# A hand-written order of work: v's copy behind the third turning's, the second exponentials behind the first, rank and x's addition between the maxima

## The chip, the cores and the metric
The kernel runs on one core of one Trainium2 chip. The metric is device time in microseconds of one execution: a median of several runs. One further execution was profiled.

## What is computed
A layer of cross attention followed by a mixture of experts, all in float32, for 16 batches of 256 tokens of width 256 and a context of 256 rows of width 192:
```python
def xattn(x, context, w_q, w_k, w_v, w_o, b_o):        # 16 heads of 64
    q, k, v = x @ w_q, context @ w_k, context @ w_v    # split into heads
    sim = einsum('bhid,bhjd->bhij', q, k) * 64 ** -0.5
    out = einsum('bhij,bhjd->bhid', softmax(sim), v)
    return out @ w_o + b_o
x = x + xattn(layernorm(x), ctx, ...)
x = x + ffn(layernorm(x), ...)
```
`ffn` takes a softmax over 8 experts, the two best of each token, a position for each token within its expert (a running count over all 4096 tokens, at most 640 per expert), an expert MLP 256 to 1024 to 256 with exact gelu, and the sum of both experts' rows weighted by the gates.

## The kernel before
**Attention part.** Work goes by *periods*: 64 of them, four to a batch, each with two pairs of heads, that is four heads (*units* 0 to 3) for all 256 queries. Batch `b` has periods `4b` to `4b + 3`; the text calls them its first to fourth. To keep float32's precision on TensorE most operands are split into a head and a rest, and a product is three products. So ScalarE copies each product out of PSUM (the head: `qh`, `kh`, `ah`, `xth`) and VectorE subtracts (the rest: `ql`, `kl`, `al`, `xtl`).

In period `m` these steps run, each on the engines named:
- `scores` (TensorE, L557): q times k for the four units into PSUM banks 0 to 3. `max0` to `max3` (VectorE, L896): one reduction for each unit. `exp0` to `exp3` (ScalarE, L739): two exponentials and two reads of the accumulated sum each, into `prob`.
- `inv0`, `inv1` (L901) and `norm0` to `norm3` (L907), VectorE: the probabilities over their sum. `inv1`, `norm2` and `norm3` run one period later.
- `turn0` to `turn3` of period `m - 1`: TensorE transposes the 256 x 256 probabilities of a unit (L573) into PSUM banks 4, 0, 1 and 4, and ScalarE copies them out into `probt` (L693). Banks 0 and 1 are those of the scores, so the turnings wait for the exponentials and the next scores wait for the copies.
- `pv` of period `m - 2`: probabilities times v (L587), copied to `ah`, its rest to `al`.
- `q`, `k` of period `m + 1` and `v` of period `m` (the last is a quarter of v, copied out by ScalarE only).
- per batch: `o` twice (the output product; VectorE adds `xin` and the sum is `x2`, L927), `xt` and `x2t` (transposes of the normalised tokens), and routing of a batch two or three behind: `ln2_stats`, `ln2`, `logits`, `bias`, `shift`, `gate` (L957 to L966), `rank` (L973 to L977), `pos` (TensorE, needs `rank`'s `chosen`), `slot`, `keys`, `pick`, and then four scatters by GpSimd to `slot_table` (L446).

**What sets the order.** Each engine runs its steps in the order of one list, `timeline()`, written by hand. An engine's queue is in order: an instruction that waits for a semaphore holds up all behind it. `xt`, `q`, `k`, `v`, `pv`, `o`, `x2t`, `logits` and `pos` share three PSUM banks (5 to 7) in turn, in the list's order, so each waits until the step three ahead of it has been read out by its last reader (`WORK_READ`; for `v` that is its copy, for `o` the addition). The wait that `scores` has on the turnings is
```python
if m >= 2:
    pe.wait_ge(sem("probt"), UNITS * (m - 2) + 3)
```
that is, the third copy of the turnings made in the period just before.

**Expert part.** After the last batch the rows of each expert are read from `slot_table`, transposed, multiplied by both weights (also split), weighted and added to the output by indirect DMAs.

Of the kernel before, what the change touches and what calls it, by code (L numbers as in the profile page):

```python
# [28 lines left out]
B, S, D = 16, 256, 256  # L29
# [4 lines left out]
ST = S // P  # L34
# [24 lines left out]
def timeline():  # L59

    out = [("ln1_stats", 0), ("ctx", 0), ("split", 0), ("ln1", 0), ("split", 1), ("xt", 0), ("q", 0), ("k", 0),
           ("split", 2), ("split", 3)]
    for m in range(PERIODS + 1):
        b, r = divmod(m, PER_B)
        live, turned, more = m < PERIODS, 1 <= m < PERIODS + 1, m + 1 < PERIODS
        out += [("scores", m), ("max0", m), ("max1", m), ("max2", m), ("max3", m), ("exp0", m)] if live else []
        scaled = [("inv1", m - 1), ("norm2", m - 1), ("norm3", m - 1)] if turned else []
        if m == PERIODS:
            out += [("ln2_stats", B - 2), *scaled]
            scaled = []  # L70
        out += [("pv", m - 2)] if m >= 2 else []
        out += [("exp1", m)] if live else []
        stats = [("ln2_stats", b - 2)] if r == 1 and 2 <= b < B else []
        if 3 <= b < B:
            out += {0: [("bias", b - 3)], 2: [("slot", b - 3)]}.get(r, [])
        if m == PERIODS - 1:
            out += [("bias", b - 2), ("shift", b - 2)]
        out += stats or scaled
        out += [("q", m + 1)] if more else []
        out += scaled if stats else []  # L80
        if 3 <= b < B:
            out += {0: [("shift", b - 3)], 2: [("keys", b - 3)]}.get(r, [])
        out += [("turn0", m - 1)] if turned else []
        out += [("exp2", m)] if live else []
        out += [("k", m + 1)] if more else []
        out += [("inv0", m), ("norm0", m), ("norm1", m)] if live else []
        out += [("turn1", m - 1)] if turned else []
        out += [("exp3", m)] if live else []

        out += {0: [("split", 4)], 1: [("split", 5)], 2: [("split", 6)], 3: [("split", 7)]}.get(m, [])  # L90
        out += [("v", m)] if live else []
        if r == 0 and b + 1 < B:
            out += [("ctx", b + 1)]
        if b == 0:
            out += {0: [("ln1_stats", 1)], 1: [("ln1", 1)]}.get(r, [])
        if 3 <= b < B:
            out += {0: [("gate", b - 3), ("rank", b - 3)], 3: [("pick", b - 3)]}.get(r, [])
        if r == 1 and 2 <= b < B:
            out += [("ln2", b - 2)]
        if r == 3 and b + 2 < B:  # L100
            out += [("ln1", b + 2)]
        out += [("turn2", m - 1)] if turned else []
        if r == (1 if b else 2) and b + 1 < B:
            out += [("xt", b + 1)]
        if r == 2 and 2 <= b < B:
            out += [("x2t", b - 2)]
        if r == 2 and b + 2 < B:
            out += [("ln1_stats", b + 2)]
        if r == 2 and 1 <= b < B:
            out += [("o", ST * (b - 1))]  # L110
        if r == 0 and 2 <= b < B:
            out += [("o", ST * (b - 2) + 1)]
        if r == 3 and 2 <= b < B - 1:
            out += [("logits", b - 2)]
        out += [("turn3", m - 1)] if turned else []
        if r == 2 and b == B - 1:
            out += [("logits", b - 2)]
        if m == PERIODS - 1:
            out += [("gate", b - 2), ("rank", b - 2), ("o", ST * (b - 1) + 1), ("pos", b - 2)]
        if r == 1 and 3 <= b < B:  # L120
            out += [("pos", b - 3)]
    last = B - 1
    out += [("slot", last - 2), ("ln2", last - 1), ("keys", last - 2), ("pick", last - 2),
            ("x2t", last - 1), ("pv", PERIODS - 1), ("logits", last - 1), ("bias", last - 1), ("shift", last - 1),
            ("gate", last - 1), ("o", ST * B - 2), ("rank", last - 1), ("o", ST * B - 1), ("ln2_stats", last),
            ("pos", last - 1), ("slot", last - 1), ("keys", last - 1), ("pick", last - 1), ("ln2", last)]
    out += [(stage, last) for stage in ("x2t", "logits", "bias", "shift", "gate", "rank", "pos", "slot", "keys",
                                        "pick")]
    assert len(set(out)) == len(out)
    return out  # L130
# [6 lines left out]


TIMELINE = timeline()
WORK_BANKS = 3  # L140

# [8 lines left out]
def build(nc, x, ctxt, wq, wk, wv, wo, bo, rw, rb, w1, b1, w2, b2, out):  # L150
    es = ExitStack()
    with es:
        sems = {}

        def sem(name):
            if name not in sems:
                sems[name] = es.enter_context(nc.semaphore("s_" + name))
            return sems[name]

        def sb(stack, name, shape, dt=F32):  # L160
            return stack.enter_context(nc.sbuf_tensor(name, [P, *shape], dt))
# [25 lines left out]
        v = sb(rest, "v", [2, ST, INNER])  # L187
# [11 lines left out]
        x2t = sb(rest, "x2t", [DC, S])  # L199
# [21 lines left out]
        rank, slot, valid, lowkey, highkey = (sb(rest, n, [ST, NE])  # L221
                                              for n in ("rank", "slot", "valid", "lowkey", "highkey"))
        chosen = sb(rest, "chosen", [ST, NE], BF16)
        before = sb(rest, "before", [NE], BF16)
        pick, same = (sb(rest, n, [2, ST]) for n in ("pick", "same"))
# [466 lines left out]
        def _(act):  # L692
# [39 lines left out]
            def exps(m, u):  # L732
                act.wait_ge(sem("max"), UNITS * m + u + 1)
                if m == 1 and u == 0:
                    act.wait_ge(sem("split_lo"), 3)
                if m >= 2:
                    act.wait_ge(sem("turn"), UNITS * (m - 2) + u + 1)
                for qb in range(ST):
                    last = act.activation(prob[:, m % 2, u, qb, :], psum[:, u, qb * S:(qb + 1) * S], ACT.Exp,  # L739
                                          bias=negmax[:, m % 2, u, qb:qb + 1],  # L740
                                          accum_out=total[:, m % 2, u, qb:qb + 1])
                last.then_inc(sem("exp"), 1)
# [27 lines left out]
            def gate(b):  # L770
                act.wait_ge(sem("shifted"), b + 1)
                act.activation(lexp[:, :, :], logit[:, :, :], ACT.Exp).then_inc(sem("gate_exp"), 1)

            steps = dict(split=split, xt=xt, q=q, k=k, v=v_, pv=pv, x2t=x2t_, gate=gate,
                         exp0=lambda m: exps(m, 0), exp1=lambda m: exps(m, 1), exp2=lambda m: exps(m, 2),
                         exp3=lambda m: exps(m, 3), turn0=lambda m: turn(m, 0), turn1=lambda m: turn(m, 1),
                         turn2=lambda m: turn(m, 2), turn3=lambda m: turn(m, 3))
# [53 lines left out]
        def _(dve):  # L831
# [62 lines left out]
            def maxima(m, u):  # L894
                dve.wait_ge(sem("scores"), UNITS * m + u + 1)
                dve.tensor_reduce(negmax[:, m % 2, u, :], psum[:, u, :].rearrange("p (q s) -> p q s", q=ST),  # L896
                                  AX.X, ALU.max, negate=True).then_inc(sem("max"), 1)

            def inverse(m, half):
                dve.wait_ge(sem("exp"), UNITS * m + 2 * (half + 1))  # L900
                dve.reciprocal(invtot[:, m % 2, 2 * half:2 * half + 2, :], total[:, m % 2, 2 * half:2 * half + 2, :])\  # L901
                   .then_inc(sem("inv"), 1)
# [94 lines left out]
            def pick_(b):  # L997

                dve.wait_ge(sem("keys"), b + 1)
                if b >= 2:  # L1000
# [8 lines left out]
                dve.tensor_copy(picki[:, b % 2, :, :], pick[:, :, :]).then_inc(sem("picks"), 1)  # L1009

            steps = dict(split=split, ln1=ln1, xt=xt, q=q, k=k, max0=lambda m: maxima(m, 0), max1=lambda m: maxima(m, 1),
                         max2=lambda m: maxima(m, 2), max3=lambda m: maxima(m, 3), pv=pv, o=o,
                         inv0=lambda m: inverse(m, 0), inv1=lambda m: inverse(m, 1),
                         norm0=lambda m: norm(m, 0), norm1=lambda m: norm(m, 1), norm2=lambda m: norm(m, 2),
                         norm3=lambda m: norm(m, 3),
# [91 lines left out]
```

## Time and profile before
| | |
|---|---|
| median of 3 runs | 1056.79 us (1056.28 to 1056.82) |
| profiled execution | 1054.35 us, span 1052.5 us |
| TensorE, matmuls | 968.4 us busy (92%) |
| TensorE, weight loads | 872.0 us (83%) |
| VectorE | 774.7 us (74%) |
| ScalarE | 628.0 us (60%) |
| GpSimd | 260.1 us (25%) |
| mean granted TensorE clock | 0.977 of full |
| batches 0 to 15 of attention | up to about 755 us |
| last routing and its scatters | to 803 us |
| experts | 803 to 1052 us |

An engine's busy time is the union of its instructions in the profiled execution. A matmul is pipelined and its recorded end is modelled, so a pause of TensorE shows somewhat shorter than the distance between two starts. In a row of busy time by stretch the numbers are the stretch and its length, then busy time (and instructions) of TensorE's matmuls, its weight loads, VectorE, ScalarE and GpSimd, the granted clock, the DMA engines' busy share and GB/s; where only TensorE was asked for, the other engines are left out. In the timeline a row is the start in us, the duration, the engine, the line, the operation with its operands, the number of instructions merged, and in brackets the idle time just before it with what ended it.

### The profile page before, as it was taken

How to read it: one execution, taken by the hardware profiler on the slowest of the kernel's cores; microseconds unless marked ns; L12 is line 12 of the kernel's file. 1: busy time of each engine (PE TensorE's matmuls, PEld its weight loads, DVE VectorE, ACT ScalarE, POOL GpSimd, SP SyncE). 2: the span in 40 equal slices, each digit the busy share in tenths (PEclk: the TensorE clock that was granted, in tenths of full speed). 3: DMA queues.
4: the chain of work that ended last, by engine and by line, in shares of the span. 5: the costliest groups of instructions: out<-in, count | busy, mean ns of one | idle time of the engine just before them, and what ended most of it. 6: DMA issues, size and time to landing. Idle time of an engine off the chain costs nothing.

```text
span 1052.5 us, 22859 instructions
## 1 busy us (share of the span) xinstructions
PE 968.4 (92%) x8224; PEld 872.0 (83%) x8224; DVE 774.7 (74%) x2096; ACT 628.0 (60%) x1738; POOL 260.1 (25%) x428
## 2 busy tenths in 40 slices
PE   4789999999999999999999999999845999999996
PEld 3678888888888888888888888888644999999996
DVE  4777778788887878788787878878663667766662
ACT  3777777766776767677766767777522334443330
POOL 2320211223131322313132231301231322222332
PEclk9899999999999999999999999999976999999998
DMA  8530101000010101011010101000024244445522
GB/s 226 149 105 2 32 1 32 22 31 23 31 51 7 39 13 31 13 31 42 2 41 6 31 8 32 16 1 15 12 97 172 60 93 124 125 125 132 132 26 26
DMA packets 47822, 56.73 MB, mean 54 GB/s; under 512 B 5228, under 2 KB 43098, under 8 KB 47584
## 3 DMA queue, kind: packets, MB, share of 16 engines
q1 hardware_dynamic: 38880, 46.30, 14.2%
q0 software_dynamic: 8832, 8.98, 5.3%
q8 instruction: 67, 1.10, 0.4%
q14 instruction: 43, 0.35, 0.1%
HBM read 36.01 MB, written 24.20 MB: 57 GB/s over the span
## 4 chain that ended last, share of the span: by engine, by line
PE 70%; ACT 12%; DVE 8%; issue 6%; DMA 1%; POOL 1%; POOLq 0%; another core or an unknown queue 0%; SPq 0%; ACTq 0%; DVEq 0%
PE psum L494 33%; PE psum L678 11%; PE psum L587 10%; PE psum L557 8%; PE psum L573 7%; ACT prob L739 6%; ACT probt L693 3%; DVE prob L907 3%; ACT kh L693 1%; PE psum L643 1%; DVE kl L844 1%; PE psum L605 1%; DVE negmax L896 1%; DMA slot_table<-row,picki 1%; ACT ah L693 1%
## 5 line engine op out<-in xcount | busy, mean ns | idle before, releaser
L739 ACT ACTIVATE prob<-psum,negmax 128x256 f32<-128x256 f32 x512 | 241.5, 489 | 98.2 <-DVE negmax L896 98.2
L693 ACT ACTIVATE probt<-psum 128x512 f32<-128x512 f32 x256 | 160.1, 631 | 41.2 <-PE psum L573 40.1
L896 DVE TENSOR_REDUCE negmax<-psum 128x2 f32<-128x512 f32 x256 | 159.0, 683 | 22.8 <-PE psum L557 22.4
L907 DVE TENSOR_SCALAR prob<-prob,invtot 128x256 f32<-128x256 f32 x512 | 160.2, 376 | 4.5
L573 PE MATMUL psum<-ident,prob 128*128 128x128 f32 x1024 | 153.2, 273 | 1.8 <-ACT probt L693 1.0
L820 ACT ACTIVATE hid<-psum,b1t 128x640 f32<-128x640 f32 x64 | 50.9, 796 | 136.3 <-PE psum L494 136.3
L573 PEld LDWEIGHTS psum<-ident,prob 128*128 128x128 f32 x1024 | 119.6, 142 | 13.9 <-issue 3.8
L587 PE MATMUL psum<-probt,v 128*64 128x256 f32 x1024 | 126.0, 389 | 0.0
L446 POOL DMA_INDIRECT slot_table<-row,picki x64 | 65.8, 1028 | 198.6 <-DVE picki L1009 171.8
L739 ACT ACTIVATION_READ_ACCUMULATOR prob<-psum,negmax 128x1 f32 x512 | 112.8, 220 | 0.0
L557 PE MATMUL psum<-kh,qh 64*128 64x256 f32 x512 | 84.1, 307 | 30.2 <-ACT probt L693 26.4
L474 POOL DMA_INDIRECT out_rows<-y,rowi x40 | 65.5, 1638 | 185.5 <-DVE y L1058 163.3
L587 PEld LDWEIGHTS psum<-probt,v 128*64 128x64 f32 x1024 | 68.5, 138 | 37.1 <-issue 1.7
L678 PE MATMUL psum<-w2h,hidh 128*128 128x256 f32 x320 | 91.1, 285 | 0.0
L678 PE MATMUL psum<-w2h,hidl 128*128 128x256 f32 x320 | 90.5, 283 | 0.0
L678 PE MATMUL psum<-w2l,hidh 128*128 128x256 f32 x320 | 90.5, 283 | 0.0
L557 PEld LDWEIGHTS psum<-kh,qh 64*128 64x128 f32 x512 | 54.7, 189 | 40.5 <-issue 40.5
L407 POOL TENSOR_SCALAR shifted<-ln_mean_var 128x2 f32<-128x2 f32 x32 | 7.2, 224 | 317.8 <-issue 300.0
L494 PE MATMUL psum<-bufh,w1h 128*128 128x320 f32 x256 | 81.4, 318 | 1.1 <-DVE bufl L844 1.1
L494 PE MATMUL psum<-xth,wqh 128*128 128x256 f32 x256 | 80.0, 312 | 1.4 <-DVE xtl L844 1.4
L494 PE MATMUL psum<-bufh,w1l 128*128 128x320 f32 x256 | 80.1, 313 | 0.0
L494 PE MATMUL psum<-bufl,w1h 128*128 128x320 f32 x256 | 80.1, 313 | 0.0
(155 smaller groups left out, 2738.8 us busy)
## 6 DMA issues: line engine op xcount, KB each, us to landing
w1r<-in_w SPq DMA_DIRECT2D x8, 1024.0 KB, 8.1
w2r<-in_w SPq DMA_DIRECT2D x8, 1024.0 KB
slot_table<-blank SPq DMA_DIRECT2D x8, 662.5 KB, 9.7
rows<-slot_table SPq DMA_DIRECT2D x8, 662.5 KB, 5.3
xin<-in_x SPq DMA_DIRECT2D x16, 256.0 KB, 2.9
out_rows<-x SPq DMA_DIRECT2D x16, 256.0 KB, 3.2
c<-in_ctxt SPq DMA_DIRECT2D x16, 128.0 KB, 3.0
c<-in_ctxt SPq DMA_DIRECT2D x32, 64.0 KB, 2.9
```

The source lines that it names most:

```text
L446: pool.indirect_dma_start(out=table, out_offset=bass.IndirectOffsetOnAxis(ap=picki[:, b % 2, k, t:t + 1], axis=0), in_=row[:, b % 2, t, :] ...
L474: pool.indirect_dma_start(out=out_rows, out_offset=bass.IndirectOffsetOnAxis(ap=rowi[:, e % 2, s:s + 1], axis=0), in_=y[:, e % 2, s, :], i ...
L494: mm = pe.matmul(dst, lhs, rhs, start=(j == 0), stop=(j == len(terms) - 1))
L557: mm = pe.matmul(psum[:, 2 * cc + h, qb * S:(qb + 1) * S], a[r, m % 2, cc, cols], w[r, m % 2, cc, :], start=(j == 0), stop=(j == len(terms ...
L573: mm = pe.transpose(psum[:, TURN_BANK[u], kb * S + qb * P:kb * S + (qb + 1) * P], prob[:, m % 2, u, qb, kb * P:(kb + 1) * P], ident[:, :])
L587: mm = pe.matmul(dst[h * HD:(h + 1) * HD, cc * S:(cc + 1) * S], v[:, b % 2, kb, cols], probt[:, m % 2, 2 * cc + h, kb, :], start=(kb == 0) ...
L678: mm = pe.matmul(dst, a[:, j, ss], w[:, j, :], start=(j == 0 and m == 0), stop=(j == HC - 1 and m == 2))
L693: copy = lambda dst, src, **kw: act.activation(dst, src, ACT.Copy, **kw)
L739: last = act.activation(prob[:, m % 2, u, qb, :], psum[:, u, qb * S:(qb + 1) * S], ACT.Exp, bias=negmax[:, m % 2, u, qb:qb + 1], accum_out ...
L820: act.activation(hid[:, at % 2, :].rearrange("p (a s) -> p a s", a=2), psum[:, 2 * (at % 2):2 * (at % 2) + 2, 0:HALF], ACT.Gelu, bias=b1t[ ...
L896: dve.tensor_reduce(negmax[:, m % 2, u, :], psum[:, u, :].rearrange("p (q s) -> p q s", q=ST), AX.X, ALU.max, negate=True).then_inc(sem("m ...
L907: last = dve.tensor_scalar(prob[:, m % 2, u, qb, :], prob[:, m % 2, u, qb, :], invtot[:, m % 2, u, qb:qb + 1], None, ALU.mult)
```

## The change
The list alone is changed, and with it the names of two steps, so that an engine's part of a step can be placed apart from TensorE's. `v` stays TensorE's product; its copy by ScalarE is now the step `v_sb`. `o` stays TensorE's product; the addition by VectorE is now the step `x2add`.
- ScalarE: the copy of v comes behind that of `turn2`, no longer ahead of it. `exp1` comes directly behind `exp0`, and pv's copy behind both.
- VectorE: `max0`, `max1`, then in the second period of a batch `rank` (before: in the first period, behind `gate`) and the addition of x for the second half of a batch's tokens (before: at the end of the first period), then `max2`, `max3`.
- The order of TensorE and GpSimd is as it was, and so is the order in which the three banks go round.

```diff
-        out += [("scores", m), ("max0", m), ("max1", m), ("max2", m), ("max3", m), ("exp0", m)] if live else []
+        out += [("scores", m), ("max0", m), ("max1", m), ("exp0", m), ("exp1", m)] if live else []
+        if r == 1 and 3 <= b < B:
+            out += [("rank", b - 3)]
+        if r == 1 and 2 <= b < B:
+            out += [("x2add", ST * (b - 2) + 1)]
+        out += [("max2", m), ("max3", m)] if live else []
...
         out += [("pv", m - 2)] if m >= 2 else []
-        out += [("exp1", m)] if live else []
...
-            out += {0: [("gate", b - 3), ("rank", b - 3)], 3: [("pick", b - 3)]}.get(r, [])
+            out += {0: [("gate", b - 3)], 3: [("pick", b - 3)]}.get(r, [])
...
         out += [("turn2", m - 1)] if turned else []
+        out += [("v_sb", m)] if live else []
...
-            out += [("o", ST * (b - 1))]
+            out += [("o", ST * (b - 1)), ("x2add", ST * (b - 1))]
...
-            out += [("gate", b - 2), ("rank", b - 2), ("o", ST * (b - 1) + 1), ("pos", b - 2)]
+            out += [("gate", b - 2), ("rank", b - 2), ("o", ST * (b - 1) + 1), ("x2add", ST * (b - 1) + 1),
+                    ("pos", b - 2)]
...
-            ("gate", last - 1), ("o", ST * B - 2), ("rank", last - 1), ("o", ST * B - 1), ("ln2_stats", last),
+            ("gate", last - 1), ("o", ST * B - 2), ("x2add", ST * B - 2), ("rank", last - 1), ("o", ST * B - 1),
+            ("x2add", ST * B - 1), ("ln2_stats", last),
...
-            steps = dict(split=split, xt=xt, q=q, k=k, v=v_, pv=pv, x2t=x2t_, gate=gate,
+            steps = dict(split=split, xt=xt, q=q, k=k, v_sb=v_, pv=pv, x2t=x2t_, gate=gate,
...
-                         max2=lambda m: maxima(m, 2), max3=lambda m: maxima(m, 3), pv=pv, o=o,
+                         max2=lambda m: maxima(m, 2), max3=lambda m: maxima(m, 3), pv=pv, x2add=o,
```

## Rows read from the trace of the kernel before
**Rows 1.** Busy time by stretch: batches 4 and 6, the experts.
```profile
200.65:245.99 45.34, 44.61 (x401) 39.13 (x402) 37.49 (x112) 33.07 (x100) 11.96 (x23) 1.00 0.09 31
...
292.39:338.71 46.32, 44.96 (x401) 39.09 (x402) 37.45 (x112) 32.70 (x100) 11.77 (x23) 1.00 0.10 30
...
803.46:1052.50 249.04, 238.02 (x1798) 237.67 (x1798) 160.05 (x289) 89.17 (x137) 65.53 (x40) 0.97 0.41 98
```

**Rows 2.** What TensorE's idle time ahead of the scores (L557) ended on.
```profile
  ACT probt L693: 26.4, 33
```

**Rows 3.** Timeline, first scores of five periods: start, us, engine, idle before.
```profile
53.77 0.38 PE L557 MATMUL psum<-kh,qh 64*128 64x256 f32 x2 [1.55 <-ACT probt L693]
...
65.07 0.39 PE L557 MATMUL psum<-kh,qh 64*128 64x256 f32 x2 [2.00 <-ACT probt L693]
...
223.11 0.39 PE L557 MATMUL psum<-kh,qh 64*128 64x256 f32 x2 [0.52 <-ACT probt L693]
...
315.83 0.39 PE L557 MATMUL psum<-kh,qh 64*128 64x256 f32 x2 [1.06 <-ACT probt L693]
...
338.71 0.38 PE L557 MATMUL psum<-kh,qh 64*128 64x256 f32 x2 [0.21 <-ACT probt L693]
```

**Rows 4.** Timeline, TensorE: turn3 before scores, scores, turn3 before scores.
```profile
304.12 0.60 PE L573 MATMUL psum<-ident,prob 128*128 128x128 f32 x4
...
304.64 0.39 PE L557 MATMUL psum<-kh,qh 64*128 64x256 f32 x2
...
337.87 0.63 PE L573 MATMUL psum<-ident,prob 128*128 128x128 f32 x4
```

**Rows 5.** Timeline, ScalarE in the second period of batch 4.
```profile
217.99 0.60 ACT L693 ACTIVATE qh<-psum 128x512 fp32r<-128x512 f32 x1
...
221.72 0.65 ACT L693 ACTIVATE v<-psum 128x512 f32<-128x512 f32 x1
...
222.19 0.66 ACT L693 ACTIVATE probt<-psum 128x512 f32<-128x512 f32 x1
```

**Rows 6.** Timeline, second period of batch 6, VectorE, ScalarE and TensorE.
```profile
306.29 0.29 DVE L973 TENSOR_TENSOR equal<-equal,lower 128x128 f32<-128x128 f32 x1
...
307.69 2.48 DVE L896 TENSOR_REDUCE negmax<-psum 128x2 f32<-128x512 f32 x4
...
308.40 0.48 ACT L739 ACTIVATE prob<-psum,negmax 128x256 f32<-128x256 f32 x1 [3.05 <-DVE negmax L896]
...
309.32 0.60 ACT L693 ACTIVATE ah<-psum 128x512 fp32r<-128x512 f32 x1
...
310.04 0.36 PE L494 MATMUL psum<-c0h,wkh 128*128 128x256 f32 x1
...
312.40 1.14 DVE L907 TENSOR_SCALAR prob<-prob,invtot 128x256 f32<-128x256 f32 x4
...
313.16 0.63 PE L573 MATMUL psum<-ident,prob 128*128 128x128 f32 x4
...
314.40 0.68 ACT L693 ACTIVATE v<-psum 128x512 f32<-128x512 f32 x1
...
314.88 0.69 ACT L693 ACTIVATE probt<-psum 128x512 f32<-128x512 f32 x1
```

**Rows 7.** Timeline, q's copy and the fourth scatter, batches 4 and 6.
```profile
205.89 0.60 ACT L693 ACTIVATE qh<-psum 128x512 fp32r<-128x512 f32 x1
...
206.16 1.09 POOL L446 DMA_INDIRECT slot_table<-row,picki  x1 [0.30 <-issue]
...
297.59 0.97 POOL L446 DMA_INDIRECT slot_table<-row,picki  x1 [0.30 <-issue]
...
299.40 0.60 ACT L693 ACTIVATE qh<-psum 128x512 fp32r<-128x512 f32 x1 [1.43 <-remote]
```

**Rows 8.** Granted clock (PEclk) behind the waits of 1.55 and 2.00.
```profile
53.80:57.20 3.40, 3.40 (x40) 1.00 1.12 313
...
65.10:68.50 3.40, 3.40 (x28) 0.55 0.03 7
```

## What the change will do to the time
> **What bounds the kernel now.** I read the page first, then the busy time by batch, then what each engine's idle time ended on, then the timeline of single periods. TensorE is the bound of the attention part: within one batch of it (45.34 or 46.32 us) TensorE is busy for 44.6 to 45.0 us, VectorE for 37.5 and ScalarE for 33 [rows 1]. What can be won there is TensorE's idle time. The waits name it: the scores of a period wait for ScalarE to have copied a turned tile out of PSUM, 26.4 us in 33 waits [rows 2]. The code says which copy: `scores` wants `UNITS * (m - 2) + 3` copies, which is that of turn2, the third turning. Rows 3 show the kinds: 1.55 and 2.00 us in the first batch, 0.52 in batch 4, and from batch 5 to 14 twice a batch, 1.06 before the third period and 0.21 before the first. The expert part (249 us, TensorE 96% busy) follows later and shares none of this [rows 1].
>
> **Swap of the v copy and turn2's copy.** Today ScalarE copies v, then turn2's tile. The two copies start 0.47 to 0.48 us apart [rows 5, 6]. When the turning has ended before the v copy starts, putting v behind makes turn2's copy that much earlier. In batch 4 the v copy starts at 221.72 and turn2's copy at 222.19; the copy takes 0.66 and the scores start 0.26 after its end, at 223.11 [rows 3, 5]. With the swap they start at 222.63: 0.48 of the 0.52 is gone. The v copy itself gets no waiter: its bank is next used three products later, and pv wants it two periods on. The copy of turn3 comes at the same place as before in ScalarE's order of three, so pv isn't later.
> Seven waits at the ends of periods in the first three batches (all at least 0.62 long; two of them stand in [rows 3]) lose 0.48 each: 3.4 us. One of 0.38 at the end of batch 2 goes: 0.4. In batches 3 and 4 the wait of 0.52 loses 0.48. The wait of 0.21 before a batch's first scores is really longer: turning to scores takes 0.84 (337.87 to 338.71) against 0.52 where nothing is late (304.12 to 304.64) [rows 3, 4], so it hides 0.11 in the draining array, and 0.32 goes. Two batches at 0.80: 1.6. Batch 15 has the same pair in smaller form: 0.7.
> **The clock.** After the gap of 1.55 us the granted clock was 1.00 over the next 3.4 us; after that of 2.00 us it was 0.55 [rows 8], the lower level (1.2 GHz) for most of the stretch. The loss is 0.45 x 3.4 = 1.5 us. The swap shortens the gap of 2.00 to 1.52, below the one that kept the full level. I count 1.5, and keep nothing as the lower bound. The two longer gaps near the start lose no clock time by my count: one is shortened by only 0.48 out of 4, the other has nothing to do with the copy.
>
> **Rank and x's addition between the maxima.** In the second period of a batch VectorE starts rank at 306.29 and max0 at 307.69: 1.40 us in front of it (four small operations of rank, then the addition) [rows 6]. ScalarE waited 3.05 us for that max0 and began exp0 at 308.40. Moved behind max1, they leave max0 and max1 1.40 earlier, and max2 and max3 where they were. So exp0, exp1, turn1 and all of ScalarE's queue behind come earlier, while VectorE's own total is unchanged. What is late next is VectorE: norm2 starts at 312.40, behind max3, pv's subtraction, the statistics and q's subtraction, and turn2 starts on TensorE at 313.16, right behind its first normalisations [rows 6]. Both stay where they are, if VectorE's queue does. Turn2's transposes then end at 313.79, its copy runs directly, to 314.45, and the scores start at about 314.7 in place of 315.83: 1.1 us.
> The Trainium skill, page "SBUF — State Buffer", section "SBUF: two separate sides", says that a VectorE operation with two SBUF inputs waits while GpSimd holds the port pair they share. Two of rank's operations are of that kind and now lie in front of max2. No row here prices such a wait; it would be on VectorE alone, so the sum stays by either, and it only makes the first rival somewhat likelier.
>
> **exp1 directly behind exp0.** Today pv's copy lies between. One unit of exponentials takes 0.92 (308.40 to 309.32) [rows 6], and pv's transposed product ends later than exp0. So exp1 fills a wait. One unit more, and pv's copy comes 1.84 after exp0's start, which by my count is when pv's product ends. In the first period of batches 5 to 14 it matters: q's copy there waits 1.43 us for something that the profile calls remote (299.40) [rows 7]. In batch 4 the same copy ran at once, at 205.89. The difference that I see is GpSimd's fourth scatter: in batch 4 the copy began 0.27 before it (206.16); in batch 6 q's product ended just as it began (297.59). With the scores of a batch 0.32 earlier against VectorE's pick, which starts the scatters, q ends about 0.3 ahead of the fourth one again, as in batch 4. So I expect the late q copy to vanish, and with it what it makes late: k's subtraction, the normalisations, gate, and so VectorE's whole second period. What that is worth is read off as the difference of the two batches: 46.32 - 45.34 = 0.98 [rows 1]. If it stays, the bound from the other side is 0 for this part.
> Ten batches (5 to 14) then save 0.98 + 0.48 + 0.32 = 1.78, which is 17.8; I take 17.4, since the rows beside batch 6 are up to 0.1 shorter than it.
>
> **Sum.** 3.4 + 0.4 + 1.6 + 0.7 + 1.5 + 17.4 = 25.0 us. Against the profiled execution (span 1052.5, time 1054.35) that is a span of 1027.5 and 1029.3. The median of the runs shown is 1056.79, 2.4 above, and 25.0 off it gives 1031.8. The tail after the last period and the experts are only shifted: their order on VectorE and TensorE is the same, and their waits (rows of the table, scatter) are chains of their own.
>
> **Rivals.**
> 1. *The second period stays VectorE's.* The late q copy stays (it may be tied to the scatters in some other way), VectorE's queue of the second period is where it was, and turn2 waits for norm2 as today. Then ten batches save only 1.1 each: 25.0 - 17.4 + 11.2 = 18.8 us, 1038.0. For it: VectorE has no idle row from 306.29 to the next maxima. Against: batch 4.
> 2. *Only the swap pays.* Moving rank gives ScalarE time, but a wait of the same length takes its place at the third period's scores (turn3, or k's subtraction, which also stands in front of them). Ten batches save 0.48 + 0.32, and the clock isn't regained: 3.4 + 0.4 + 1.6 + 0.7 + 8.0 = 14.1, 1042.7.
> 3. *No change.* The scores really wait for something else that ends together with turn2's copy, so the earlier copy frees nothing. Against it: the waits name this copy in all 33, and the step of 0.26 from its end to the scores is the same at 223.11 and 315.83 [rows 3, 5, 6]. 1056.8.
> 4. *Slower: k's bank.* k of the second period writes the bank in which o of the batch before last still waits for x's addition. k starts at 310.04. The addition was over when max0 began, at 307.69; with max0 and max1 in front of it (half of 2.48) it is over at about 308.9 [rows 6]. It has 1.1 us to spare. Should VectorE run later by d + 1.1, each of 13 batches stalls d; above d = 1.9 us the change loses. d = 2.1 gives 1059. Nothing in the trace makes VectorE 3 us later.
>
> **Chances.** The forecast 0.50; rival 1 0.26; rival 2 0.12; no change 0.04; slower 0.04; and 0.04 that more goes than I count (the clock near the start). A measurement of this kernel can tell 0.2%, 2 us, from no change: faster 0.92, same 0.04, slower 0.04. The forecast's own range is 1029 to 1034.5. The range for 8 in 10 takes in rival 1 and the near edge of rival 2: 1028 to 1042.
>
> **What would show it.** Right: the wait of scores on probt falls from 26.4 us to about 6, most of it in the first two batches; the waits of 1.06 and 0.21 are gone from batch 5 on; a batch takes 44.6 us; in the second period exp0 starts within a microsecond of max0's product and pv's copy follows exp1; the granted clock behind the gap at 63 us is 1.00; the remote wait before qh is gone. Wrong: turn2 of the second period still starts behind norm2, or scores name VectorE (k's subtraction) as their releaser, or the q copy still waits 1.4 us, or k of the second period waits for x's addition. Then the sum falls to rival 1 or 2. The weakest step is the vanishing of the remote wait, whose cause I infer from two batches.

## The result: 1040.35 us, 1.5% faster, two thirds of the forecast gain
The changed kernel takes 1040.35 us (median of 4 runs, 1039.95 to 1041.8) against 1056.53 beside it: 16.2 us less, a ratio of 0.9849 with a 95% interval of 0.9832 to 0.9866. Its profiled execution took 1040.31 us, span 1038.5. The forecast was 25.0 us less, at 1031.8; the range of 1028 to 1042 holds the result.

Batch 6 takes 45.35 us in place of 46.32 [rows 1]; the forecast was 44.6. The experts' stretch is as long as before:
```profile
285.00:330.35 45.35, 44.92 (x402) 39.02 (x401) 37.14 (x113) 32.95 (x100) 11.76 (x23) 1.00 0.10 30
...
789.38:1038.50 249.12, 238.06 (x1799) 237.71 (x1798) 160.00 (x289) 89.08 (x137) 65.50 (x40) 0.97 0.41 98
```
The wait of the scores on the turned copies fell from 26.4 us in 33 waits [rows 2] to 7.7 in 6. Another took its place, which the list of waits before does not have: k's product waits for `valid`, an operation of slot on VectorE:
```profile
  ACT probt L700: 7.7, 6
...
PE psum L501 <- DVE valid L991: 3.0, 10, 0.3
```
The first scores behind the waits of [rows 3]: the two of the first batch are shorter by 0.49 and 0.44, and those of 1.06 and 0.21 in batch 6 are gone.
```profile
53.33 0.39 PE L564 MATMUL psum<-kh,qh 64*128 64x256 f32 x2 [1.06 <-ACT probt L700]
...
64.20 0.39 PE L564 MATMUL psum<-kh,qh 64*128 64x256 f32 x2 [1.56 <-ACT probt L700]
...
307.18 0.39 PE L564 MATMUL psum<-kh,qh 64*128 64x256 f32 x2
...
330.35 0.38 PE L564 MATMUL psum<-kh,qh 64*128 64x256 f32 x2
```
In the second period of batch 6 (compare [rows 6]) max0 and max1 come first, rank behind them; exp0 follows at once, and pv's copy stands behind both units of exponentials. Turn2's transposes still start behind norm2, their copy then runs at once, and v's comes last:
```profile
298.79 1.28 DVE L903 TENSOR_REDUCE negmax<-psum 128x2 f32<-128x512 f32 x2
...
299.51 0.47 ACT L746 ACTIVATE prob<-psum,negmax 128x256 f32<-128x256 f32 x1 [1.71 <-DVE negmax L903]
...
299.99 0.28 DVE L980 TENSOR_TENSOR equal<-equal,lower 128x128 f32<-128x128 f32 x1
...
301.32 0.61 ACT L700 ACTIVATE ah<-psum 128x512 fp32r<-128x512 f32 x1
...
304.88 1.14 DVE L914 TENSOR_SCALAR prob<-prob,invtot 128x256 f32<-128x256 f32 x4
...
305.65 0.63 PE L580 MATMUL psum<-ident,prob 128*128 128x128 f32 x4
...
306.31 0.60 ACT L700 ACTIVATE probt<-psum 128x512 f32<-128x512 f32 x1
...
306.80 0.59 ACT L700 ACTIVATE v<-psum 128x512 f32<-128x512 f32 x1
```
The third period of the same batch is what the forecast did not have. max0 starts 1.87 us behind the scores (307.18), since TensorE is earlier and VectorE not. Both units of exponentials run ahead of pv's copy, pv's subtraction waits 0.69 for that copy, slot stands behind it, and k's product starts when slot has read the bank of `pos`:
```profile
309.05 1.28 DVE L903 TENSOR_REDUCE negmax<-psum 128x2 f32<-128x512 f32 x2
...
309.76 0.47 ACT L746 ACTIVATE prob<-psum,negmax 128x256 f32<-128x256 f32 x1 [1.39 <-DVE negmax L903]
...
311.57 0.61 ACT L700 ACTIVATE ah<-psum 128x512 fp32r<-128x512 f32 x1
...
312.21 0.69 DVE L851 TENSOR_TENSOR al<-psum,ah 128x512 fp32r<-128x512 f32 x1 [0.69 <-ACT ah L700]
...
312.90 0.17 DVE L991 SCALAR_TENSOR_TENSOR valid<-psum,chosen 128x16 f32<-128x16 f32 x1
...
313.12 0.39 PE L501 MATMUL psum<-c0h,wkh 128*128 128x256 f32 x1 [0.30 <-DVE valid L991]
```
And in the first period ScalarE's copies around the fourth scatter are late as before (compare [rows 7]). q's product ends 0.29 us ahead of that scatter, as the forecast wanted, and q's copy still starts 0.7 us behind the product's end (0.04 where nothing is late). Turn0's copy then starts 1.89 us after the scatter, where q's copy started 1.81 after it in the kernel before; turn0's transposes had ended at 290.63.
```profile
290.49 1.00 POOL L453 DMA_INDIRECT slot_table<-row,picki  x1 [0.30 <-issue]
...
290.90 0.60 ACT L700 ACTIVATE qh<-psum 128x512 fp32r<-128x512 f32 x1 [1.54 <-PE psum L501]
...
292.38 0.60 ACT L700 ACTIVATE probt<-psum 128x512 f32<-128x512 f32 x1 [0.88 <-PE psum L580]
```
The granted clock (PEclk) behind the shortened wait of 1.56 us is the full one, where it was 0.55 [rows 8]. In the routing behind the last period it is at the lower level for a time, where the kernel before had 1.00 at the same step:
```profile
64.20:67.60 3.40, 3.40 (x40) 1.00 0.01 2
...
747.60:750.60 3.00, 3.00 (x14) 0.52 0.00 0
```

Where the time went, from the starts of the first scores of each period in the profiled executions (us):

| part | before | changed | difference | forecast |
|---|---|---|---|---|
| start to the first scores | 19.95 | 21.51 | +1.56 | 0 |
| batches 0 to 2 | 135.36 | 129.02 | -6.34 | -5.3 |
| batches 3 and 4 | 90.68 | 89.38 | -1.30 | -1.6 |
| batches 5 to 14 | 462.40 | 453.17 | -9.23 | -17.4 |
| batch 15 up to its last scores | 36.00 | 35.39 | -0.61 | -0.7 |
| from there to the end | 308.16 | 310.05 | +1.89 | 0 |

Of the 6.34 us in batches 0 to 2, 1.46 are luck with the clock: the second period of the first batch took 13.21 us before and 11.75 changed. Behind a pause of TensorE of 2.07 us in both, the granted clock was 0.53 before and 1.00 changed. The other profiles show how far chance goes there: the first three batches take 127.5 to 131.4 us in the nine profiles with the swap and 134.8 to 136.4 in the four without it.

### The profile page after: what moved, and what is told of

It reads as the page before. It is cut to its first block, busy times and chain, and to the rows that moved or that the text cites. A ratio compares the mean times of both kernels' runs of the same rounds, so it can differ in the third digit from the quotient of the medians.

```text
span 1038.5 us, 22859 instructions
## 1 busy us (share of the span) xinstructions
PE 967.7 (93%) x8224; PEld 870.3 (84%) x8224; DVE 768.6 (74%) x2096; ACT 628.4 (61%) x1738; POOL 259.0 (25%) x428
## 4 chain that ended last, share of the span: by engine, by line
PE 67%; DVE 18%; ACT 6%; issue 5%; DMA 2%; POOL 1%; SPq 0%; POOLq 0%; ACTq 0%; DVEq 0%
PE psum L501 34%; PE psum L685 11%; PE psum L594 7%; PE psum L580 7%; PE psum L564 6%; DVE prob L914 5%; ACT prob L746 4%; DVE negmax L903 3%; DVE al L851 1%; DVE kl L851 1%; ACT probt L700 1%; PE psum L650 1%; DVE stats L858 1%; DVE row L867 1%; PE psum L612 1%
## 5 line engine op out<-in xcount | busy, mean ns | idle before, releaser
L746 ACT ACTIVATE prob<-psum,negmax 128x256 f32<-128x256 f32 x512 | 238.9, 483 | 82.3 <-DVE negmax L903 82.3
L700 ACT ACTIVATE probt<-psum 128x512 f32<-128x512 f32 x256 | 157.1, 615 | 50.7 <-PE psum L580 48.9
L914 DVE TENSOR_SCALAR prob<-prob,invtot 128x256 f32<-128x256 f32 x512 | 163.9, 384 | 4.5
L827 ACT ACTIVATE hid<-psum,b1t 128x640 f32<-128x640 f32 x64 | 50.9, 795 | 136.4 <-PE psum L501 136.4
L453 POOL DMA_INDIRECT slot_table<-row,picki x64 | 65.8, 1028 | 196.9 <-DVE picki L1016 170.2
L746 ACT ACTIVATION_READ_ACCUMULATOR prob<-psum,negmax 128x1 f32 x512 | 110.7, 216 | 0.0
L564 PE MATMUL psum<-kh,qh 64*128 64x256 f32 x512 | 80.5, 305 | 11.8 <-ACT probt L700 7.7
L501 PE MATMUL psum<-woh,ah 128*128 128x256 f32 x256 | 74.9, 293 | 0.5 <-DVE al L851 0.5
```

Of the source, the lines that this page charges most:

```text
L453: pool.indirect_dma_start(out=table, out_offset=bass.IndirectOffsetOnAxis(ap=picki[:, b % 2, k, t:t + 1], axis=0), in_=row[:, b % 2, t, :] ...
L501: mm = pe.matmul(dst, lhs, rhs, start=(j == 0), stop=(j == len(terms) - 1))
L564: mm = pe.matmul(psum[:, 2 * cc + h, qb * S:(qb + 1) * S], a[r, m % 2, cc, cols], w[r, m % 2, cc, :], start=(j == 0), stop=(j == len(terms ...
L700: copy = lambda dst, src, **kw: act.activation(dst, src, ACT.Copy, **kw)
L827: act.activation(hid[:, at % 2, :].rearrange("p (a s) -> p a s", a=2), psum[:, 2 * (at % 2):2 * (at % 2) + 2, 0:HALF], ACT.Gelu, bias=b1t[ ...
L914: last = dve.tensor_scalar(prob[:, m % 2, u, qb, :], prob[:, m % 2, u, qb, :], invtot[:, m % 2, u, qb:qb + 1], None, ALU.mult)
```

## Experiments
Each time is a ratio to the kernel before, run beside it, with its 95% interval. The edits of swap_only, rank_only and exp1_only are shown against the kernel before, that of norm_ahead against no_exp1, the others against the changed kernel; the two renamed steps are in all of them. The table gives the mean length of the four periods in batches 5 to 14 and the sum of these ten batches, from each kernel's profiled execution.

| kernel | 1st | 2nd | 3rd | 4th | ten batches |
|---|---|---|---|---|---|
| before | 12.30 | 11.06 | 12.54 | 10.35 | 462.4 |
| changed | 12.11 | 10.04 | 13.10 | 10.07 | 453.2 |
| swap_only | 12.10 | 10.70 | 12.54 | 10.07 | 454.1 |
| rank_only | 12.20 | 10.35 | 12.54 | 10.34 | 454.3 |
| exp1_only | 12.24 | 10.93 | 12.76 | 10.34 | 462.8 |
| no_exp1 | 12.10 | 9.98 | 12.54 | 10.07 | 446.9 |
| changed_again | 12.11 | 10.15 | 13.10 | 10.07 | 454.3 |
| slot_first | 12.10 | 10.12 | 12.54 | 10.07 | 448.3 |
| exp1_third | 12.11 | 10.06 | 12.53 | 10.07 | 447.8 |
| two_scatters | 12.10 | 9.86 | 12.66 | 10.07 | 446.9 |
| norm_ahead | 12.10 | 9.91 | 13.13 | 10.07 | 452.1 |

**swap_only.** Rank, x's addition and exp1 are put back; only the copies change places.
```diff
         out += [("turn2", m - 1)] if turned else []
+        out += [("v_sb", m)] if live else []
...
-            steps = dict(split=split, xt=xt, q=q, k=k, v=v_, pv=pv, x2t=x2t_, gate=gate,
+            steps = dict(split=split, xt=xt, q=q, k=k, v_sb=v_, pv=pv, x2t=x2t_, gate=gate,
```


> Of the change only v's copy behind turn2's copy. If the prediction's term is right, the early periods give 3.4 + 1.5 (clock) + 0.4, batches 3 and 4 1.6, batches 5 to 14 0.48 in the second period and 0.3 in the fourth, 7.6, and batch 15 0.7: 15 us in all, 1041.5. If the swap pays only where the turning ends before ScalarE comes free, it is 8 to 9 (1048). In the third period k does not wait for VectorE in either case.


Measured: 0.9862 (0.9843 to 0.9882), 1038.3 us, 15.8 less than before. The swap alone gives what the whole change gives, and its term was sized right (15): the first three batches give 5.5 us, the ten batches 8.3. The rows are the second period of its batch 6: the turning was over 0.6 us before the copy began, and the scores follow the copy's end by 0.25.
```profile
304.56 0.63 PE L577 MATMUL psum<-ident,prob 128*128 128x128 f32 x4
...
305.81 0.69 ACT L697 ACTIVATE probt<-psum 128x512 f32<-128x512 f32 x1
...
306.75 0.39 PE L561 MATMUL psum<-kh,qh 64*128 64x256 f32 x2 [0.58 <-ACT probt L697]
```

**rank_only.** Only rank and x's addition move.
```diff
-        out += [("scores", m), ("max0", m), ("max1", m), ("max2", m), ("max3", m), ("exp0", m)] if live else []
+        out += [("scores", m), ("max0", m), ("max1", m), ("exp0", m)] if live else []
+        if r == 1 and 3 <= b < B:
+            out += [("rank", b - 3)]
+        if r == 1 and 2 <= b < B:
+            out += [("x2add", ST * (b - 2) + 1)]
+        out += [("max2", m), ("max3", m)] if live else []
...
-            out += {0: [("gate", b - 3), ("rank", b - 3)], 3: [("pick", b - 3)]}.get(r, [])
+            out += {0: [("gate", b - 3)], 3: [("pick", b - 3)]}.get(r, [])
```


> Of the change only rank and x's addition between the maxima. ScalarE's queue of the second period comes earlier, so that turn2's copy is behind v's but no longer behind VectorE's delay: 0.8 a batch in batches 5 to 14 and nothing before batch 3, 8 to 9 us, 1048. If VectorE's queue is all that counts, nothing comes of it alone: 1056.


Measured: 0.9937 (0.9921 to 0.9954), 1047.2 us, 6.9 less. In the profiled execution the ten batches give the forecast 8.1 us, and the first three take 1.0 more. The second period falls by 0.71, with v's copy still ahead of turn2's:
```profile
314.55 0.65 ACT L700 ACTIVATE v<-psum 128x512 f32<-128x512 f32 x1
...
315.03 0.65 ACT L700 ACTIVATE probt<-psum 128x512 f32<-128x512 f32 x1
...
315.94 0.39 PE L564 MATMUL psum<-kh,qh 64*128 64x256 f32 x2 [0.27 <-ACT probt L700]
```

**exp1_only, and exp1_only_again.** Only exp1 moves, ahead of pv's copy.
```diff
-        out += [("scores", m), ("max0", m), ("max1", m), ("max2", m), ("max3", m), ("exp0", m)] if live else []
+        out += [("scores", m), ("max0", m), ("max1", m), ("exp0", m), ("exp1", m)] if live else []
+        out += [("max2", m), ("max3", m)] if live else []
...
-        out += [("exp1", m)] if live else []
```


> Of the change only exp1 directly behind exp0. My theory: it gives nothing anywhere, since pv's copy waits for TensorE or comes at the same time, and it costs where VectorE's maxima are late against pv: 1056.5, within 2 us. The rival, that it takes q's copy out of the wait called remote and so frees the second period, gives 5 to 10 us.

> exp1 directly behind exp0 alone, a second time, since the first time's profile was 0.4 us shorter than before's and its runs 4.7 us longer. If the profile tells it, 0.998 to 1.002 of before; if the runs do, 1.003 to 1.007.


Measured: 1.0055 (1.0038 to 1.0072), and the second time 1.0044 (1.0029 to 1.006): slower by about 5 us. The part is a loss, not nothing, and the first expectation missed it. Of that the periods show little: the ten batches are 0.4 and, in the second profile, 0.9 longer; the third period is longer by 0.22 in both, and the first two give some of it back. The second profiled execution (1059.06 us) has 1.3 us more before the first scores and 2.8 behind the last. The first of these is not exp1's: it is ScalarE's wait for the DMA of the first weights, 7.4 us in place of 5.6. Most of this part's own 5 us stays unexplained.

**no_exp1, and no_exp1_again.** The whole change with exp1 left behind pv's copy.
```diff
-        out += [("scores", m), ("max0", m), ("max1", m), ("exp0", m), ("exp1", m)] if live else []
+        out += [("scores", m), ("max0", m), ("max1", m), ("exp0", m)] if live else []
...
         out += [("pv", m - 2)] if m >= 2 else []
+        out += [("exp1", m)] if live else []
```


> The whole change but for exp1, which stays behind pv's copy. My theory: in the third period k waits for the bank of pos, read by slot on VectorE, behind pv's subtraction, behind pv's copy, behind exp1; without the move the wait of 0.3 (0.57 by starts) in 11 batches goes: 6 us less than the changed kernel, 1034.3. The rival, that the wait comes from TensorE being earlier against VectorE's maxima and exp1 has no part in it, gives 1040.3.

> The swap and the move of rank and x's addition, exp1 behind pv's copy, a second time: 0.981 of before, 4 to 6 us below the changed kernel. If the first time owed it to the chip, it is 0.985.


Measured: 0.9808 (0.9789 to 0.9827) and 0.9806 (0.9783 to 0.9829), 1032.9 and 1033.7 us. It beats both kernels, and a batch takes 44.7 us, where the forecast was 44.6. In its third period of batch 6 (scores at 306.29) pv's copy runs between the units, pv's subtraction finds it done, and k's product starts 5.40 behind the scores with no wait, against 5.94 in the changed kernel:
```profile
309.91 0.60 ACT L701 ACTIVATE ah<-psum 128x512 fp32r<-128x512 f32 x1
...
310.55 0.68 DVE L852 TENSOR_TENSOR al<-psum,ah 128x512 fp32r<-128x512 f32 x1
...
311.23 0.17 DVE L992 SCALAR_TENSOR_TENSOR valid<-psum,chosen 128x16 f32<-128x16 f32 x1
...
311.69 0.36 PE L502 MATMUL psum<-c0h,wkh 128*128 128x256 f32 x1
```

**slot_first.** exp1 stays in front; only slot, on VectorE, goes ahead of pv's subtraction in the third period.
```diff
+        if r == 2 and 3 <= b < B:
+            out += [("slot", b - 3)]
         out += [("pv", m - 2)] if m >= 2 else []
...
-            out += {0: [("bias", b - 3)], 2: [("slot", b - 3)]}.get(r, [])
+            out += {0: [("bias", b - 3)]}.get(r, [])
```


> The changed kernel with slot ahead of pv's subtraction on VectorE in the third period, exp1 still ahead of pv's copy. My theory (k waits for the bank that slot reads, and slot stands behind pv's subtraction and so behind exp1): the third period falls from 13.1 to 12.54 us, 5 to 6 us less than the changed kernel beside it. The rival (exp1 makes k's own operands or turn0 late): 13.1 stays.


Measured: 0.9811 (0.9781 to 0.9842), 1036.2 us, 5.2 less than the changed kernel beside it. The subtraction still waits for pv's copy (0.53), but `valid` is ahead of it, and the third period is 12.54:
```profile
309.31 0.17 DVE L993 SCALAR_TENSOR_TENSOR valid<-psum,chosen 128x16 f32<-128x16 f32 x1
...
309.37 0.61 ACT L702 ACTIVATE ah<-psum 128x512 fp32r<-128x512 f32 x1
...
310.01 0.69 DVE L853 TENSOR_TENSOR al<-psum,ah 128x512 fp32r<-128x512 f32 x1 [0.53 <-ACT ah L702]
...
310.37 0.36 PE L503 MATMUL psum<-c0h,wkh 128*128 128x256 f32 x1
```
This settles the path: exp1, pv's copy, pv's subtraction, slot, the bank, k. Nothing else that exp1 delays counts in that period. The whole runs' intervals overlap with the changed kernel's; it is the third period (12.53 or 12.54 in all ten batches, 12.97 to 13.12 in the changed kernel) that tells them apart.

**exp1_third.** exp1 behind pv's copy in the third periods only.
```diff
-        out += [("scores", m), ("max0", m), ("max1", m), ("exp0", m), ("exp1", m)] if live else []
+        out += [("scores", m), ("max0", m), ("max1", m), ("exp0", m)] if live else []
+        out += [("exp1", m)] if live and r != 2 else []
...
+        out += [("exp1", m)] if live and r == 2 else []
```


> The changed kernel with exp1 behind pv's copy in the third period of each batch only. If exp1 costs only there, this is 6 us less than the changed kernel, as slot_first; if it also costs behind the last batch or in the other periods, it keeps those 1 to 2 us against the kernel with exp1 behind pv's copy everywhere (0.981 of before).


Measured: 0.9817 (0.9792 to 0.9842), 1036.7 us. The third period is mended. Against no_exp1 nothing can be told: the intervals overlap.

**changed_again.** The control on the same chip as slot_first, exp1_third and two_scatters.


> The changed kernel once more, beside the others of this group on one chip: 0.985 of the time before, with the third period at 13.1 us from batch 5 on. What of its time lies in the routing behind the last period (1.9 us more than before in the first profile, with a lower granted clock there) is either in it again, or was one execution's.


Measured: 0.9857 (0.9833 to 0.9881), 1041.3 us. The stretch from the last scores to the end is 310.04 us, again near the 310.05 of the first profile. But it was 308.0 and 312.2 in the two profiles of no_exp1, and 308.2 and 311.0 in the two with exp1 alone. So it is the execution more than the list that sets it. The granted clock differs there too: these profiles have the lower level at other steps of that routing. How much of the difference is the clock's was not separated. The second period has a mean of 10.15 us here and 10.04 in the first profile, so 0.1 us in that column is no more than one execution against another.

**two_scatters.** Two of the four scatters of each batch are left out, with the counts that wait for them; each token's second expert gets no row.
```diff
-                for k in range(2):
+                for k in range(1):
```


> The changed kernel with two of the four scatters of each batch left out (each token's second expert gets no row). My theory: the copy behind the fourth scatter (turn0's in the first period of batches 5 to 14) no longer starts 1.8 to 1.9 us behind it; q's copy starts 5.2 us after the batch's scores and k's subtraction at about 8 in place of 9.4, and the second period falls from 10.04 to 9.86. The rival, that the delay has another cause (the engine's own instruction supply), leaves 9.4 and 10.04.


Measured: 1028.2 us in one execution, span 1026.4. In batch 6 (scores at 285.52) q's copy starts at 5.24 behind the batch's scores and turn0's at 5.73, where the changed kernel had 5.90 and 7.38; k's copy comes at 7.11 in place of 8.77, k's subtraction at 8.46 (expected about 8, 9.41 in the changed kernel), and the second period is 9.86.
```profile
288.44 0.97 POOL L453 DMA_INDIRECT slot_table<-row,picki  x1 [0.30 <-issue]
...
290.76 0.60 ACT L700 ACTIVATE qh<-psum 128x512 fp32r<-128x512 f32 x1 [0.87 <-PE psum L501]
...
291.25 0.59 ACT L700 ACTIVATE probt<-psum 128x512 f32<-128x512 f32 x1
...
292.63 0.61 ACT L700 ACTIVATE kh<-psum 128x512 fp32r<-128x512 f32 x1
```
So the delay of ScalarE belongs to the third and fourth scatters, and the prediction's idea of the cause was right, but not its idea of how it is escaped. What the delay costs is told less well. GpSimd's own work behind the scatters (the addition to `xin`) starts 2.6 us earlier here, at 5.46 behind the batch's scores in place of 8.02, so the 0.18 us of the second period may be due to either. The third period is shorter too (12.66), and the stretch from the last scores to the end is 6.6 us shorter than in the changed kernel.

**norm_ahead.** no_exp1 with inv1, norm2 and norm3 ahead of q's subtraction, the statistics behind it.
```diff
-        out += stats or scaled
+        out += scaled
         out += [("q", m + 1)] if more else []
-        out += scaled if stats else []
+        out += stats
```


> The same, and in the second period inv1, norm2 and norm3 ahead of q's subtraction and the statistics on VectorE. If turn2's wait for norm2 is what is left of that period (9.98 in place of 9.86), it falls to 9.86 and 1 us goes. The rival: the statistics come 1.6 us later, GpSimd's root and with it ln2 hold VectorE by 0.5 us in front of the next maxima, and nothing is won, or up to 5 us lost.


Measured: 0.9873 (0.9857 to 0.9888), 1038.4 us, 4.7 more than no_exp1_again beside it (7 by the ratios). The second period falls to 9.91, and the third rises to 13.13: its max0 starts 2.50 us behind the scores, and k waits for slot again. The rival was right: VectorE has to come to slot in time, and whatever makes it late there is paid by TensorE.

## Why the prediction was right in sign and too large
The range of 1028 to 1042 holds 1040.35, but near its upper end, which was there for rivals 1 and 2, and none of the rivals had exp1's loss, which brought the time there. That it holds is in part luck. In the profiles of batches 5 to 14 the swap gives 8.3 us, rank and x's addition on top of it 7.2, and exp1 takes 6.3 back.
- *The swap.* Right, in mechanism and size: seven early waits lost 0.40 to 0.53 each, those of batches 3 to 14 went but for at most 0.07, and swap_only gives 15.8 us where its terms come to 15. It alone is as large as the change's net gain.
- *The clock.* Right: 1.56 us of idle kept the full clock where 2.00 had lost it; the period behind it took 9.85 in place of 11.88. All nine profiles with the swap have 1.56 to 1.59 us there and a granted clock of 1.00, all four without it 1.99 or 2.00 us and 0.55 to 0.65 over the next 3.4 us. The length of the pause alone is no rule: 2.07 us ahead of the second period of the first batch was followed by 1.00 in the changed kernel, and 3.54 us ahead of the third period of slot_first's, behind a period that began at 0.57, by 1.00 as well.
- *Rank and x's addition.* Right in mechanism: alone 6.9 us; on top of the swap the second period falls from 10.70 to 9.98. Turn2 then starts behind norm2, as the step said. (The prediction's list of signs calls the same thing a sign of being wrong; its two places don't agree.) The rule of the Trainium skill, page "SBUF — State Buffer", section "SBUF: two separate sides", had nothing to act on in batch 6: rank's four operations take 1.05 us (299.99 to the addition at 301.04), as before, but GpSimd has no instruction in that stretch. Batch 4 of no_exp1 agrees with the rule: with GpSimd's subtraction beside it, rank's first operation takes 0.71 us.
```profile
209.13 0.74 POOL L406 TENSOR_TENSOR c0l<-c,c0h 128x256 fp32r<-128x256 f32 x1
...
209.30 0.71 DVE L981 TENSOR_TENSOR equal<-equal,lower 128x128 f32<-128x128 f32 x1
```
- *exp1 directly behind exp0.* This step failed. The term of 17.4 us came out at 9.2, and most of what it lacks is here. "So exp1 fills a wait" was worked out with maxima that are on time. In the third period the change itself makes TensorE early against VectorE's maxima (1.87 us from scores to max0, 0.98 before); exp0 then starts late, exp1 does not fill the wait for pv but lengthens it, and the 0.9 us reach k by way of a bank that I followed for x's addition and for v, and not for pos. No_exp1 has its max0 as late there (1.86 us) and loses nothing. The move costs 0.56 us in each third period, and with small amounts in the second 6.3 over the ten batches (446.9 against 453.2), of the 8.2 that the term of 17.4 lacks. In the kernel before, the same move costs those periods 0.22 (max0 is 1.53 us behind the scores there).
- *The held copy.* "So I expect the late q copy to vanish" failed, though its condition was met: q's product ends 0.29 us ahead of the fourth scatter, and q's copy still comes at 5.90 in place of 5.24. Turn0's copy is held longer, to 7.38. In batches 12 to 14 q's copy itself comes 1.1 to 1.9 us behind the scatter's start. The queue behind is only 0.1 earlier (k's copy 8.77 behind the batch's scores, 8.88 before), and VectorE's not at all: norm2 of the second period starts 7.78 us behind its scores, 7.75 before. So the 0.98 us a batch, read off as the difference of batches 6 and 4, did not come in whole. The second period is 10.04 where two_scatters has 9.86, 1.8 us over ten batches; 0.6 of these are counted above for exp1, and that all of the rest is the held copy's is not shown.
- *Rival 1* described the second period rightly (turn2 behind norm2, VectorE full). Its 18.8 us come near the 16.2 by luck: it counts 1.1 us a batch and leaves out the 0.32 ahead of a batch's first scores, which its own condition doesn't touch. With it the sum is about 22 us, and no_exp1, which has its mechanism and not exp1's loss, gives 15.5 us in the ten batches.
- *The ends.* 1.6 us before the first scores and 1.9 behind the last, in the one profile, were in no term. Both differ about as much between executions of one kernel (exp1_only and its second profile: 19.73 and 21.22 before the first scores, no_exp1 and its second: 308.0 and 312.2 behind the last). At the start it is the DMA of the first weights, for which ScalarE waits 7.3 us in the changed kernel's profile and 5.6 in that of before.

## What to carry to other kernels
Cost a reordering against the queues as they stand after its other parts, not against the old trace: exp1's move cost the old third periods 0.22 us and the new ones 0.56, once TensorE had become early. Where a few banks go round, look up for every step the last reader of the bank it takes, and everything ahead of that reader on its engine. And take the parts of a change apart once: here the swap alone gave all of the net gain, two parts together 4 to 5 us more than the three.

## What the runs showed of the hardware
While GpSimd works on the third and fourth scatters of a batch and shortly behind them, ScalarE's waits on products of TensorE end late. From batch 5 to 14 q's copy in the kernel before starts 1.80 to 1.91 us after the fourth scatter's start, 0.8 to 0.9 us behind the scatter's recorded end, though its product had ended as the scatter began. In the changed kernel turn0's copy starts 1.87 to 1.92 us after it, in nine of these ten batches; in the tenth (batch 13) it is again q's, 1.85 after. Exponentials whose maxima were long there ran in the same stretch without delay (batch 4, 206.93 to 207.95). Without the third and fourth scatters the copies start 0.04 to 0.1 us after the product. What in the scatter holds them is not shown.

VectorE's operations with two inputs in SBUF take longer beside GpSimd's work on SBUF: rank's first one 0.71 us beside a subtraction in batch 4 of no_exp1, 0.28 with GpSimd idle. This also makes single periods long. In batch 7 of no_exp1 GpSimd's work on the next context comes late, two of gate's operations take 0.70 and 0.75 us in place of 0.22, and the second period takes 10.73 us, where six of batches 5 to 14 have 9.85 or 9.86: max0 of that period comes 0.9 us later than in batch 9.
